# A two-layer recurrent and attention block: the first set-up reordered, k split by 128 channels in layer two, one relu moved

## The chip, the cores and the metric

One Trainium2 chip, one core. The metric is the device time of one execution in microseconds (us). TensorE (PE) multiplies, VectorE (DVE), ScalarE (ACT) and GpSimd (POOL) work on elements, SyncE (SP) issues most of the DMAs.

## The reference

Input x is 4 x 2048 rows of 256 channels. Two layers follow, each `x = x + s * silu(g)` with xn the layernorm of x.

Layer one, s: receptance, key and value are products of a mix of xn and the row before it with Wr, Wk, Wv; a recurrence runs over time for each channel:

```python
mo = jnp.maximum(m, kk + u)
e1 = jnp.exp(m - mo)
e2 = jnp.exp(kk + u - mo)
out = (e1 * num + e2 * vv) / (e1 * den + e2)
ms = jnp.maximum(m + w, kk)
e1s = jnp.exp(m + w - ms)
e2s = jnp.exp(kk - ms)
```

Then `sigmoid(receptance) * out` times Wo. Layer one, g: `relu(xn @ W1 + b1) @ W2 + b2` with 1024 hidden channels.

Layer two, s: latent attention with 16 heads of 16 channels and 8 rotary ones: c_q and c_kv are products of xn to 64 channels, q, k and v come from them, the scores are clipped and causal, and the result is multiplied by W_O. Layer two, g: `sigmoid(xr @ W_r) * (relu(xk @ W_k)^2 @ W_v)`, xr and xk being mixes of xn with its previous row.

## The kernel before

The 8192 rows are handled in 16 chunks of CH = 512 (4 to a batch row). The program has four stages, one after another: layer one with its set-up (0 to about 620 us), the projections of layer two with their set-up (to about 932), attention (to about 1940), and the output product. Each engine has its own instruction list, written out by hand, and waits on counting semaphores; the order in a list is the order of execution. Nearly all products are made of float16 halves: an operand is scaled and copied to a high half on ScalarE, and the rest, operand minus high half, is the low half, mostly on VectorE; a product is three matmuls (high x high, high x low, low x high).

Set-up of layer one. POOL computes the reciprocal deviation of each row (rstd_of). DVE squares and sums the three mixed weights (sum_squares), PE adds the sums over partitions with a product by ones (L804), ACT takes the root (L323), DVE makes the scales from it. Only then come, in ACT's list, normalise(0, 0) (four instructions, L382), xn_of(0, 0) (copies out of the transposed rows in ps_t: L346, and four of prev, L360), three weight_high (L333), two mixed_high (L375), and four squares with sums of the other weights (L455), whose sum over partitions (PE, L813) leads to a second root (L457) and second scales. DVE's list has xn_low_of(0, 0) (L522), mix(0) (four instructions, L511), weight_low 0 to 2 (L527), and two mixed_low (L517). PE's list: norm product L804, transposes(0) (L744), the receptance product behind w_low 3, norm product L813, key, value.

One chunk of layer one. ACT's chunk() takes the sigmoid of the receptance, then hidden(n, m), the relu of one of eight groups of 128 hidden channels (L399), with the three exponentials (L394; new, old, bonus) between them, and hidden_high (L404), the high halves. PE makes hidden product m into one of two halves of ps_a, so product m waits for relu m - 2. POOL makes the eight low halves (hidden_low, L278) and then the numerator's product with the sigmoid (L284). DVE runs keys() and states() with the scans over time (L544, L567 the denominator, L571 the numerator), takes rwkv (L696) and its low half (L699), which PE's output product (ps_out) waits for, and finishes the rows (L711, L713).

One chunk of layer two's projections. PE: latents, k of the relu branch (ps_b, behind xk_low), kr, qc, qr, transposes of the next chunk, receptance with k's up-projection in its middle (ps_c, `kc_mm`), values, and the squared-relu product (L1551), which waits for `kc_low` since it writes ps_c again. ACT: qc's high half (L1298), xn_of of the next chunk (L1236, prev copies L1250), with keys_high (L1302) in between. DVE: qr parts (L1442), layernorm statistics (L1338), k's low half (L1447), aggregate (L1345), xn's low half (L1350), mix (L1359), xk's low half (L1364), qr's low half (L1457), gate input (L1462). SP stores qc, kr, kc, qr, v and the gate in this order.

## Time and profile before

| | |
|---|---|
| Median of 3 runs | 2000.93 us (2000.35 to 2001.17) |
| Profiled execution | 2001.22 us, span 1999.5 us |
| PE busy in the span | 1893.0 us (95%) |
| DVE busy | 1765.7 us (88%) |
| ACT busy | 1710.3 us (86%) |
| POOL busy | 536.6 us (27%) |

The shares are means over stages with different limits, so they say little on a change in one stage. A row of a timeline gives the start in us from the span's start, how long it took, the engine, the line, the operation with its output and inputs, how many instructions are merged (xN), and in brackets how long the engine stood idle before it and who ended that.

### The profile page before, as it was taken

The page shows a single profiled execution, that of the slowest core. Times are in us where ns is not written, and L with a number is a line of the kernel's source. Part 1 is how long each engine was busy: PE and PEld are TensorE (multiplying, and loading weights), DVE is VectorE, ACT ScalarE, POOL GpSimd, SP SyncE. Part 2 cuts the span into 40 slices and gives each one's busy share as a digit, 9 for nine tenths or more (in the row PEclk, how much of TensorE's full clock was granted, in tenths as well). Part 3 has the DMA queues.
Part 4 walks back from the last instruction along what each step waited for, and adds up shares of the span by engine and source line. Part 5 has one row for each costly group of instructions (what it writes and reads, how often), then busy time and mean ns, then how long its engine had stood idle before and what let it go on. Part 6 is the DMA issues. An engine that isn't in the chain of part 4 may idle for free. (4 is left out here: it accounts for less than half of the span.)

```text
span 1999.5 us, 53552 instructions
## 1 busy us (share of the span) xinstructions
PE 1893.0 (95%) x22950; PEld 979.8 (49%) x22950; DVE 1765.7 (88%) x2361; ACT 1710.3 (86%) x2137; POOL 536.6 (27%) x426
## 2 busy tenths in 40 slices
PE   3899999999995999998999999999999999999988
PEld 1465665666653665664344433444344444344437
DVE  5999999999996888885898999989999899998976
ACT  6777877778775888886999999999999999999970
POOL 0564554646544676663000000000000000000003
PEclk9999999999997999998999999999999999999999
DMA  3001001010112465566222222222222222221329
GB/s 109 22 22 43 22 22 43 22 43 22 54 43 79 159 197 189 191 168 207 69 74 56 68 67 71 75 56 68 67 72 76 55 68 52 58 66 42 82 83 342
DMA packets 130221, 166.25 MB, mean 83 GB/s; under 512 B 13632, under 2 KB 101696, under 8 KB 129728
## 3 DMA queue, kind: packets, MB, share of 16 engines
q1 hardware_dynamic: 127952, 160.59, 27.3%
q8 instruction: 180, 2.95, 0.6%
q10 hardware_dynamic: 2032, 2.24, 0.3%
q14 instruction: 57, 0.47, 0.1%
HBM read 91.21 MB, written 71.57 MB: 81 GB/s over the span
## 5 line engine op out<-in xcount | busy, mean ns | idle before, releaser
L1771 ACT ACTIVATE c_probs<-c_ps_b 128x1536 f32<-128x1536 f32 x544 | 892.3, 1640 | 0.0
L1899 PE MATMUL c_ps_o<-c_probs,c_v 128*32 128x256 f32 (+3 forms) x6656 | 582.5, 453 | 3.7 <-DVE c_probs L1817 0.5
L1817 DVE TENSOR_SCALAR c_probs<-c_probs 128x2048 f32<-128x2048 f32 (+2 forms) x415 | 432.8, 1054 | 38.2 <-ACT c_probs L1771 36.2
L1879 PE MATMUL c_ps_b<-c_qk 24*128 24x256 f16 (+2 forms) x8064 | 459.8, 294 | 5.7 <-PEq L1099 5.7
L1879 PE MATMUL c_ps_a<-c_qk 24*128 24x256 f16 (+2 forms) x2688 | 449.9, 294 | 6.4 <-ACT c_probs L1770 4.9
L1770 ACT ACTIVATE c_probs<-c_ps_a 128x512 f32<-128x512 f32 x544 | 422.8, 777 | 2.5 <-PE c_ps_a L1879 2.5
L1879 PEld LDWEIGHTS c_ps_b<-c_qk 24*128 24x128 f16 x8064 | 222.7, 93 | 332.6 <-ACT c_probs L1771 243.9
L2052 POOL TENSOR_TENSOR d_prod<-d_prod,d_x 128x1024 f32<-128x1024 f32 x4 | 9.4, 2350 | 1025.5 <-DVE d_prod L2041 1025.5
L1899 PEld LDWEIGHTS c_ps_o<-c_probs,c_v 128*32 128x32 f32 x6656 | 161.7, 109 | 245.8 <-issue 146.6
L278 POOL TENSOR_TENSOR a_hidh<-a_hid,a_hidh 128x512 f16<-128x512 f32 x128 | 205.1, 1629 | 152.7 <-ACT a_hidh L404 152.7
L1879 PEld LDWEIGHTS c_ps_a<-c_qk 24*128 24x128 f16 x2688 | 199.4, 93 | 18.0 <-ACT c_probs L1770 15.3
L733 PE MATMUL a_ps<-a_xnh,a_w 128*128 128x512 f16 x768 | 175.6, 381 | 16.3 <-ACT a_hid L399 11.7
L1822 DVE TENSOR_SCALAR c_probs<-c_probs 128x1536 f32<-128x1536 f32 (+2 forms) x208 | 165.3, 801 | 28.5 <-ACT c_probs L1771 27.8
L733 PE MATMUL a_ps<-a_w,a_hidh 128*128 128x256 f16 x1536 | 171.3, 273 | 4.8 <-POOL a_hidh L278 4.8
L1826 DVE SCALAR_TENSOR_TENSOR c_probs<-c_probs,c_caps 128x512 f32<-128x512 f32 x256 | 169.5, 682 | 0.0
L733 PEld LDWEIGHTS a_ps<-a_w,a_hidh 128*128 128x128 f16 x1536 | 149.7, 98 | 27.4 <-POOL a_hidh L278 4.8
L733 PEld LDWEIGHTS a_ps<-a_xnh,a_w 128*128 128x128 f16 x768 | 71.8, 97 | 117.4 <-ACT a_hid L399 30.8
L399 ACT ACTIVATE a_hid<-a_ps,a_b 128x512 f32<-128x512 f32 x128 | 86.2, 688 | 18.9 <-PE a_ps L733 15.3
L733 PE MATMUL a_ps<-a_xnh,a_wr 128*128 128x512 f16 x384 | 87.5, 384 | 10.3 <-DVE a_wv L527 10.3
L1778 DVE STREAM_TRANSPOSE c_otok<-c_ps_o 128x512 f32<-128x512 f32 x64 | 45.9, 717 | 35.1 <-PE c_ps_o L1899 35.1
L404 ACT ACTIVATE a_hidh<-a_hid 128x512 f16<-128x512 f32 x128 | 75.2, 625 | 0.0
L375 ACT ACTIVATE a_xmixh<-a_xmix 128x1024 f16<-128x1024 f32 x32 | 33.8, 1057 | 40.6 <-DVE a_xmix L511 40.6
(278 smaller groups left out, 2795.9 us busy)
## 6 DMA issues: line engine op xcount, KB each, us to landing
v_d<-b_val SPq DMA_DIRECT2D x16, 1024.0 KB
c_v<-v_d SPq DMA_DIRECT2D x64, 256.0 KB
rows<-in_x SPq DMA_DIRECT2D x16, 512.0 KB, 4.8
x_d<-rows_out SPq DMA_DIRECT2D x16, 512.0 KB, 3.2
rows<-x_d SPq DMA_DIRECT2D x16, 512.0 KB, 5.1
qc_d<-b_qc SPq DMA_DIRECT2D x16, 512.0 KB
kc_d<-b_kc SPq DMA_DIRECT2D x16, 512.0 KB
gate_d<-rows_out SPq DMA_DIRECT2D x16, 512.0 KB, 3.3
```

The costliest lines, as they stand in the source:

```text
L278: nc.gpsimd.tensor_tensor(hid_half[:, 1, m], hid[:, m % RING], hid_half[:, 0, m], ALU.subtract).then_inc(hid_low, 1)
L399: nc.scalar.activation(hid[:, m % RING, :], ps_a[:, m % 2, :], ACT.Relu, bias=b_1[:, m:m + 1], scale=hid_scale).then_inc(hid_done, 1)
L404: nc.scalar.activation(hid_half[:, 0, m], hid[:, m % RING], ACT.Copy).then_inc(hid_high, 1)
L733: mm = nc.tensor.matmul(ps, l, r, start=(first and i == 0), stop=(last and i == len(steps) - 1))
L1770: nc.scalar.activation(probs[:, t % NPROB, PARTS[0]], ps_a[:], ACT.Exp, scale=unscale).then_inc(exp_a_done, 1)
L1771: nc.scalar.activation(probs[:, t % NPROB, PARTS[1]], ps_b[:, t % 2], ACT.Exp, scale=unscale).then_inc(exp_b_done, 1)
L1778: nc.vector.transpose(o_tok[:, e % 2].rearrange("p k r -> p (k r)"), ps_o[:]).then_inc(tok_done, 1)
L1817: nc.vector.tensor_scalar(tile, tile, P_MAX, P_MIN, ALU.min, ALU.max).then_inc(clip_done, 1)
L1822: nc.vector.tensor_scalar(tile[:, :, at:end], tile[:, :, at:end], P_MAX, P_MIN, ALU.min, ALU.max)
L1826: op = nc.vector.scalar_tensor_tensor(tile[:, :, at:at + P], tile[:, :, at:at + P], P_MIN, cap, ALU.max, ALU.min)
L1879: mm = nc.tensor.matmul(into, k[rows, hk, kt * P:(kt + 1) * P], tokens[rows, hq], start=(i == 0), stop=(i == len(TERMS) - 1), tile_positio ...
L1899: mm = nc.tensor.matmul(ps_o[j * VW:(j + 1) * VW, column:column + w], v[:, kt, j * VW:(j + 1) * VW], probs[:, step % NPROB, j, at:at + w], ...
```

## The change

Three places. In the set-up of layer one, ACT's root of the first norms comes after normalise(0, 0), PE's transposes(0) before the first norm product, DVE's weight_low(0) before mix(0), and PE's receptance waits for one low half of weights instead of three. In each chunk of layer one, relu 3 and one high half come ahead of the bonus exponential on ACT. In each chunk of layer two, the up-projection of k signals after each 128 channels, its high and low halves are taken per 128 channels, ACT's after one copy of prev instead of two, DVE's ahead of the next layernorm statistics; xn's low half moves ahead of the aggregation.

```diff
--- before.py
+++ after.py
@@ -319,9 +319,6 @@
                 act.dma_start(raw_1, a["W1"].rearrange("(k p) d -> p k d", p=P)).then_inc(ffn_loaded[0], 16)
                 act.dma_start(raw_2, a["W2"].rearrange("(m p) d -> p m d", p=P)).then_inc(ffn_loaded[1], 16)
 
-                act.wait_ge(sums_done, 1)
-                nc.scalar.activation(roots[:, 0:VAL], ps_a[:, 0, 0:VAL], ACT.Sqrt).then_inc(roots_done, 1)
-
                 def load(name, source):
 
                     register = act.alloc_register(name)
@@ -420,23 +417,27 @@
                     old_states(n, c)
                     if following:
                         xn_of(n + 1, c + 1)
-                    for m in range(3):
+                    for m in range(2):
                         hidden(n, m)
                         exponential(n, m)
+                    hidden(n, 2)
 
                     highs = 0
-                    for m in range(2, MT):
+                    for m in range(3, MT):
                         if first and m == MT // 2:
                             act.wait_ge(w_low, 5)
-                        if m > 2:
-                            hidden(n, m)
-                        if m in (2, 4, 5, 6):
+                        hidden(n, m)
+                        if m < MT - 1:
                             hidden_high(n, highs)
                             highs += 1
+                        if m == 3:
+                            exponential(n, 2)
                     for m in range(highs, MT):
                         hidden_high(n, m)
 
                 normalise(0, 0)
+                act.wait_ge(sums_done, 1)
+                nc.scalar.activation(roots[:, 0:VAL], ps_a[:, 0, 0:VAL], ACT.Sqrt).then_inc(roots_done, 1)
                 xn_of(0, 0)
                 act.wait_ge(scale_done, 1)
                 for i in range(3):
@@ -637,8 +638,9 @@
                 dve.wait_ge(bound_done, 2)
                 scales(slice(WR, W1), 2)
                 xn_low_of(0, 0)
+                weight_low(0)
                 mix(0)
-                for i in range(3):
+                for i in (1, 2):
                     weight_low(i)
                 mixed_low(0, 0)
                 mixed_low(0, 1)
@@ -798,16 +800,16 @@
                                           first=(m == 0 and j % 2 == 0), last=(m == MT - 1 and j % 2 == 1))
                     mm.then_inc(ffn_done, 1)
 
+                pe.wait_ge(small_loaded, 16 * 5)
+                transposes(0)
                 pe.wait_ge(consts_set, 5)
-
                 pe.wait_ge(squares_done, VAL)
                 nc.tensor.matmul(ps_a[:, 0, 0:VAL], ones[:], sums[:, 0:VAL], start=True, stop=True).then_inc(sums_done, 1)
-                pe.wait_ge(small_loaded, 16 * 5)
-                transposes(0)
 
                 pe.wait_ge(roots_done, 1)
+                pe.wait_ge(w_low, 1)
+                receptance(0, 0)
                 pe.wait_ge(w_low, 3)
-                receptance(0, 0)
                 pe.wait_ge(mix_done, len(MIXED) * KT)
                 pe.wait_ge(act_squared, COLUMNS - W1)
                 nc.tensor.matmul(ps_t[:, 0, 0:COLUMNS - W1], ones[:], sums[:, W1:], start=True, stop=True).then_inc(sums_done, 1)
@@ -1116,7 +1118,7 @@
                                  qc[:, s].rearrange("p h m t -> p (h m) t")).then_inc(stored[s], 16)
                     sp.wait_ge(kr_low, n + 1 + 1)
                     sp.dma_start(d["kr"][b, :, :, t].rearrange("h p t -> p h t"), kr[:, s]).then_inc(stored[s], 16)
-                    sp.wait_ge(kc_low, n + 1)
+                    sp.wait_ge(kc_low, KT * n + KT)
                     sp.dma_start(d["kc"][b, :, :, t].rearrange("h (m p) t -> p (h m) t", p=P),
                                  kc[:, s].rearrange("p h m t -> p (h m) t")).then_inc(stored[s], 16)
                     sp.wait_ge(qr_low, n + 1)
@@ -1249,8 +1251,8 @@
                         for k in range(KT):
                             nc.scalar.activation(prev[:, i, k, 1:CH + 1], ps_t[:, k, :], ACT.Copy,
                                                  scale=mix_prev[:, i, k:k + 1]).then_inc(prev_done, 1)
-                        if i and between:
-                            between()
+                            if i and k == 0 and between:
+                                between()
 
                 def xk_high_of(n, first=False):
                     act.wait_ge(mix_done, 2 * KT * n + KT)
@@ -1298,8 +1300,9 @@
                     nc.scalar.activation(qc[:, s, 0], ps_c[:], ACT.Copy, scale=q_factor).then_inc(qc_high, 1)
 
                     def keys_high():
-                        act.wait_ge(kc_mm, n + 1)
-                        nc.scalar.activation(kc[:, s, 0], ps_c[:], ACT.Copy, scale=k_factor).then_inc(kc_high, 1)
+                        for m in range(KT):
+                            act.wait_ge(kc_mm, KT * n + m + 1)
+                            nc.scalar.activation(kc[:, s, 0, m], ps_c[:, m], ACT.Copy, scale=k_factor).then_inc(kc_high, 1)
 
                     if left >= 1:
                         xn_of(n + 1, c + 1, keys_high)
@@ -1441,16 +1444,18 @@
                         dve.wait_ge(qr_mm, 2 * n + i + 1)
                         nc.vector.scalar_tensor_tensor(t_q[:], ps_a[:, i, :], factor[:, WQ:WQ + 1], table[:, t],
                                                        ALU.mult, ALU.mult).then_inc(qr_parts, 1)
+                    for m in range(KT):
+                        dve.wait_ge(kc_high, KT * n + m + 1)
+                        nc.vector.scalar_tensor_tensor(kc[:, s, 1, m], ps_c[:, m], factor[:, WUK:WUK + 1], kc[:, s, 0, m],
+                                                       ALU.mult, ALU.subtract).then_inc(kc_low, 1)
                     if left >= 2:
                         layernorm(n + 2, c + 2, b + (c + 2) // XS)
-                    dve.wait_ge(kc_high, n + 1)
-                    nc.vector.scalar_tensor_tensor(kc[:, s, 1], ps_c[:], factor[:, WUK:WUK + 1], kc[:, s, 0],
-                                                   ALU.mult, ALU.subtract).then_inc(kc_low, 1)
+                    if left >= 1:
+                        xn_low_of(n + 1)
                     if left >= 2:
                         dve.wait_ge(stats_done, TPC * (n + 2) + TPC)
                         aggregate(n + 2)
                     if left >= 1:
-                        xn_low_of(n + 1)
                         mix(n + 1, c + 1)
                         xk_low_of(n + 1)
                     dve.wait_ge(qr_high, n + 1)
@@ -1533,8 +1538,7 @@
                         if j == TPC // 2:
                             pe.wait_ge(qc_low, n + 1)
                             for m in range(KT):
-                                mm = products(ps_c[:, m, :], [(lambda h: w_uk[:, h, m * P:(m + 1) * P], lambda h: lat[:, 1])], both)
-                            mm.then_inc(kc_mm, 1)
+                                products(ps_c[:, m, :], [(lambda h: w_uk[:, h, m * P:(m + 1) * P], lambda h: lat[:, 1])], both).then_inc(kc_mm, 1)
                         mm = tokens(ps_r[:, j, :], xr_half, w_r, j)
                     mm.then_inc(r_mm, 1)
 
@@ -1543,7 +1547,7 @@
                         mm = products(ps_val[:, j, :], [(lambda h: lat[:, 1, j * P:(j + 1) * P], lambda h: w_uv[:, h])], ((0, 0), (0, 1)))
                     mm.then_inc(val_mm, 1)
 
-                    pe.wait_ge(kc_low, n + 1)
+                    pe.wait_ge(kc_low, KT * n + KT)
                     pe.wait_ge(act_done, n + 1)
                     pe.wait_ge(late_loaded, 48)
                     for j in range(TPC):
```

## Rows read from the trace of the kernel before

**Rows 1.** Busy us by engine (PE, PEld, DVE, ACT, POOL) in two stretches
```profile
80.00:120.00 40.00, 39.44 (x258) 24.79 (x256) 38.92 (x48) 32.37 (x47) 21.49 (x15) 1.00 0.09 27
720.00:760.00 40.00, 39.23 (x222) 24.07 (x222) 32.34 (x51) 32.82 (x47) 26.73 (x23) 1.00 0.56 186
```

**Rows 2.** Timeline of the set-up: start, us, engine, line, instructions, idle before
```profile
9.01 1.28 ACT L323 ACT_TABLE_LOAD   x1 [9.01 <-DMA rows_out<-in_WvT]
13.24 0.56 PE L804 MATMUL a_ps<-a_sums,a_ones 128*128 128x3 f32 x2 [13.24 <-DVE a_sums L596]
13.91 2.07 ACT L382 ACTIVATE a_xhat<-rows,a_shift,a_rstd 128x256 f32<-128x256 f32 x4
16.13 1.94 PE L744 MATMUL a_ps<-ident,a_xhat 128*128 128x128 f32 x8 [2.33 <-ACT a_xhat L382]
18.28 1.01 ACT L346 ACTIVATE a_xnh<-a_ps 128x1024 f16<-128x1024 f32 x1
23.01 2.72 DVE L511 SCALAR_TENSOR_TENSOR a_xmix<-a_ps,a_mix_now,a_prev 128x512 f32<-128x512 f32 x4
28.34 7.07 PE L733 MATMUL a_ps<-a_xnh,a_wr 128*128 128x512 f16 x24 [10.27 <-DVE a_wv L527]
31.83 0.18 ACT L455 ACTIVATION_READ_ACCUMULATOR a_hid<-a_rwkv 128x1 f32 x1
35.57 0.17 ACT L457 ACTIVATE a_roots<-a_ps 128x4 f32<-128x4 f32 x1 [3.56 <-PE a_ps L813]
```

**Rows 3.** Timeline, layer one: low half of rwkv, output product's first matmuls
```profile
80.50 1.22 DVE L699 TENSOR_TENSOR a_rwkvh<-a_rwkv,a_rwkvh 128x1024 f16<-128x1024 f32 x1
81.87 2.78 PE L733 MATMUL a_ps<-a_wo,a_rwkvh 128*128 128x256 f16 x24
115.95 1.22 DVE L699 TENSOR_TENSOR a_rwkvh<-a_rwkv,a_rwkvh 128x1024 f16<-128x1024 f32 x1
117.47 0.71 PE L733 MATMUL a_ps<-a_wo,a_rwkvh 128*128 128x256 f16 x5
578.72 1.23 DVE L699 TENSOR_TENSOR a_rwkvh<-a_rwkv,a_rwkvh 128x1024 f16<-128x1024 f32 x1
```

**Rows 4.** Timeline of one steady chunk of layer one
```profile
232.94 6.77 PE L733 MATMUL a_ps<-a_xnh,a_w 128*128 128x512 f16 x30
238.06 1.06 ACT L394 ACTIVATE a_eb<-a_eb 128x1024 f32<-128x1024 f32 x1
238.83 1.26 DVE L567 TENSOR_TENSOR_SCAN a_den<-a_eo,a_den,a_en 128x512 f32<-128x512 f32 x1
239.52 1.27 ACT L399 ACTIVATE a_hid<-a_ps,a_b 128x512 f32<-128x512 f32 x2
240.01 2.12 DVE L571 TENSOR_TENSOR_SCAN a_num<-a_eo,a_num,a_nv 128x512 f32<-128x512 f32 x1
240.27 4.08 PE L733 MATMUL a_ps<-a_xnh,a_w 128*128 128x512 f16 x18 [0.57 <-ACT a_hid L399]
241.39 1.69 POOL L278 TENSOR_TENSOR a_hidh<-a_hid,a_hidh 128x512 f16<-128x512 f32 x1 [0.34 <-ACT a_hidh L404]
```

**Rows 5.** Layer two: timeline of one chunk, then a line of the waits
```profile
743.28 1.27 ACT L1250 ACTIVATE b_prev<-b_ps,b_mix_prev 128x512 f32<-128x512 f32 x2
744.43 1.02 ACT L1302 ACTIVATE b_kc<-b_ps 128x1024 f16<-128x1024 f32 x1
745.49 1.28 DVE L1447 SCALAR_TENSOR_TENSOR b_kc<-b_ps,b_factor,b_kc 128x1024 f16<-128x1024 f32 x1
746.83 3.72 PE L1551 MATMUL b_ps<-b_wv,b_actk 128*128 128x256 f32 x16 [0.39 <-DVE b_kc L1447]
750.78 1.22 DVE L1364 TENSOR_TENSOR b_xkh<-b_xk,b_xkh 128x1024 f16<-128x1024 f32 x1
752.98 2.75 PE L1489 MATMUL b_ps<-b_xkh,b_wk 128*128 128x512 f16 x12
...
PE b_ps L1551 <- DVE b_kc L1447: 6.1, 16, 0.4
```

## The prediction

> **What bounds the kernel now.** I read the busy time by stretch first, then the set-up and one chunk of each layer in order of time. In the chunks of layer one TensorE is busy 39.44 of 40 us and VectorE 38.92; in those of layer two TensorE 39.23 of 40, with VectorE at 32.34 [rows 1]. Both loops stand on TensorE, with VectorE close behind in layer one only. The set-up is another regime: one chain that runs through ScalarE, VectorE and TensorE in turn [rows 2]. Attention and the output stage are not touched; I take their lengths as fixed and shift them. The sum is made against the profiled execution, 2001.22 us (span 1999.5); the median of the runs shown is 2000.93, so 0.3 us comes off at the end. A difference of 0.2% is 4 us, about what a measurement can tell from none.
>
> **Set-up of layer one.** Now: ScalarE's table is loaded at 9.01 + 1.28 = 10.29, but the four normalisations sit behind the square root that waits for the weight norms, and start at 13.91. The transposes run from 16.13 to 18.07, and the copy out of them starts at 18.28 [rows 2].
> Changed: the normalisations start at 10.3, 3.6 earlier. The transposes follow by the same 2.22 us, 12.5 to 14.5. The first norm product is now behind them: it starts near 14.35 instead of 13.24, and as ScalarE went on 0.67 after its start (13.91), it now has done the root by 15.0. The copies start at 15.2 instead of 18.28: 3.1 earlier. The later root costs nothing, since the scales it feeds are first used behind those copies, over 3 us later.
> Then the order on VectorE: the low half of the receptance weights (1.2 us, as the like instruction of 1.28 in [rows 5] with its 0.1 of overlap) moves ahead of the mix, so the mix, at 23.01, starts only 3.1 - 1.2 = 1.9 earlier. ScalarE's two copies of the mix and its squares follow it back to back, so the squares' end, 31.83 + 0.19, comes at 30.1. The receptance product (28.34, 7.07 us) needs only one weight now: it can start at 23.01 - 3.1 + 1.2 + 0.2 = 21.3 and ends at 28.4. Today the second norm product waits for that receptance (28.34 + 7.07 = 35.4, root at 35.57); afterwards it waits for the squares, so the root comes at 30.1 + 0.4 = 30.5. **Gain 5.0 us**, not the 7 that TensorE alone would show: what is late next are the squares. From the second root to the first chunk's sigmoid ScalarE has one unbroken queue, which shifts as a whole.
> Bounds: 4.7 if that tiny product takes the 0.67 of the first; 5.3 if I misplace one semaphore. An extra table load is possible, 1.28 us by the row. It would lie between 12.4 and 15.0, where ScalarE waits anyway: nothing; 1.3 if it came behind the wait.
> The Trainium skill (ScalarE: Activation LUTs, Table sets: the hidden batching unit) has the cheap functions in every set and the root in one of its own, which speaks for that extra load. Another section of the page (Step-by-step: what each stage is for) gives about 2.7 us for a load with its drain; by that the root would come 0.1 later, by the row's 1.28 not at all.
>
> **Relu 3 ahead of the bonus exponential.** In each steady chunk TensorE stands 0.57 us ahead of the sixth hidden product, for relu 3 [rows 4]. Five products take 6.77 us, 1.35 each, and end at 239.71; ScalarE starts relu 3 only at 239.52, behind the bonus exponential (238.06) and one high half, 1.46 us together. Moved ahead, relu 3 waits for its own product, the fourth, which ends at 238.36, and starts near 238.5; its reader can go 0.75 later (239.52 to 240.27 now), so that wait is gone. What is late next: relu 4, now behind high half and exponential. A relu costs 0.58 (two take 1.27): relu 4 starts at 238.5 + 0.58 + 1.46 = 240.54 and lets the seventh product go at 241.3, 0.2 to 0.3 after the sixth ends. TensorE gets 0.3 to 0.4 a chunk.
> It can't keep them. The output product waits for the low half of rwkv from VectorE. It started 1.37 us after that instruction's start where TensorE was early (80.50, 81.87), and 1.52 after it one chunk on (115.95, 117.47): only 0.15 of slack. And the one interval that begins with an early TensorE is 35.45 us (80.50 to 115.95); the 13 that follow, from 115.95 to 578.72, are 35.60 each [rows 3]. So VectorE's own loop is 35.45, and the gain is 0.15 x 13 = **1.9 us**. Bounds: 0, if the late relu 4 or a low half on GpSimd eats it; 5, if VectorE's loop got shorter too, for which no row speaks. In the first chunk and the last, VectorE and GpSimd bound these steps: nothing.
>
> **Layer two, k by halves.** TensorE stands 0.39 us a chunk ahead of the squared-relu product (L1551), for the low half of k; the waits come to 6.1 us in 16 [rows 5]. ScalarE takes k's high half at 744.43, after two copies of prev (1.15 for both), and VectorE the low half from 745.49 to 746.77. Changed: after one copy, at 743.86, the first 128 channels (I take 0.48 us to the next and 0.58 to its end, by half of the 1.02), done at 744.44. VectorE's halves start at 744.5 and 745.16, at 0.66 each, as the mix's instructions of that kind and size (2.72 for four, [rows 2]); they end at 745.9. The product can then start when TensorE is free, at 746.83 - 0.39 = 746.44: all 0.39 go, with 0.5 to spare.
> What is late next: VectorE. It filled the time up to 745.49 with the next rows' statistics; now it first waits for the half (0.36 more than it waits now), pays 0.12 for the second instruction, and the statistics follow. The low half of xn passes the aggregation and gains nothing, the mix gets nearly 0.5 later, and so does the low half of x_k: 750.78 + 0.46 + 1.22 = 752.46. Its reader, now at 752.98, moves to 752.59. It fits with 0.13, less some 0.06 for the semaphore. The 0.1 more on ScalarE lies in its waits. The store of k waits for both halves on SP's queue, behind kr's store, which GpSimd releases microseconds after them: nothing. All waits go: **6.1 us**. Bounds: 3, if each VectorE step comes 0.2 later than I place it; 6.5 at most.
>
> **The sum.** 5.0 + 1.9 + 6.1 = 13.0; 2001.2 - 13.0 - 0.3 = 1987.9, say 1988.0.
>
> **The rivals.**
> A: VectorE's delay in layer two takes the gain. If the low half of x_k comes 0.4 late, the new wait replaces the one removed and layer two gives 0 to 2: 1988.0 + 5 = 1993. For it: a margin of 0.07. Against: it needs an error of four times the steps I leave open.
> B, on the other side: the turns of GpSimd and VectorE flip in layer one. A scan alone takes 1.26; the first scan of the numerator takes 2.12 and the low half on GpSimd after it 1.69: they run one behind the other [rows 4]. Now low half 1 asks at 241.39 and starts in fact when the first scan is through, at 242.1 less 0.1. Its high half comes 0.45 later with the change, so it asks at 241.85. The point is 242.0: past it the second scan goes first, and GpSimd's whole chain ends one scan later, with the product for rwkv at its end, on which VectorE waits. 14 x 1.1 = 15.4 us come back: 1988.0 + 1.9 + 15.4 = 2005. Against: 0.15 us or more of margin in a loop that repeats itself to 0.02.
> The Trainium skill (SBUF — State Buffer, Terms) has these two engines share a port pair that is held for a whole instruction, the loser fully blocked. By that rule, the trace agrees (2.12 is the rest of a low half and then a scan). If they only shared bandwidth, no flip could happen and 2005 would fall away.
> C: TensorE's 0.3 to 0.4 a chunk in layer one are kept, as VectorE's loop shortens too: 13 x 0.2 more, 1985.
> D: the set-up gives less, since the normalisations still wait (a table load behind the root's wait, late statistics): the 5.0 fall to 1.2 to 3.7, and the time is 1990 to 1992.
>
> **The numbers.** Forecast 0.66 (its own range 1986.3 to 1990.3, by the bounds of its parts); A 0.12; B 0.07; C 0.06; D 0.05; something in attention's phase or at the joins of stages that I can't price 0.04. For eight in ten I reach to C and to A: 1985.5 to 1993. Faster by over 0.2% (under 1996.9): all but B and half of the last, less a little for A with D together, 0.88; within 0.2%: 0.04; slower: 0.08.
>
> **What would show it.** Set-up: normalisation at 10.3, receptance at 21.3, second root at 30.5. Layer one: no 0.57 wait before the sixth hidden product, one of 0.2 to 0.3 before the seventh, intervals of 35.45 throughout, and GpSimd's low half 1 still behind the first scan. Layer two: no wait at L1551, intervals of 17.4 instead of 17.8, and x_k's low half ending just ahead of its product. I am wrong if a wait for VectorE stands before the x_k product, if the intervals of layer one stay at 35.60 or exceed it, or if the second root comes after 31.

## The result and the profile after

The changed kernel takes 1986.1 us (median of 4 runs: 1984.7, 1984.8, 1987.5 and 1987.9) where the kernel before takes 2000.6: ratio 0.9929, 95% interval 0.9914 to 0.9944, so 14.5 us less. The forecast was 1988.0 with a range of 1985.5 to 1993. The profiled execution took 1984.83 us (span 1983.1), 16.4 less than the one profiled before.

**Set-up.** The timeline of the changed kernel, ScalarE's rows first, then TensorE's (columns as in [rows 2]):

```profile
9.10 1.28 ACT L379 ACT_TABLE_LOAD   x1 [9.10 <-issue]
10.40 2.08 ACT L379 ACTIVATE a_xhat<-rows,a_shift,a_rstd 128x256 f32<-128x256 f32 x4
12.49 1.28 ACT L440 ACT_TABLE_LOAD   x1
14.81 0.17 ACT L440 ACTIVATE a_roots<-a_ps 128x3 f32<-128x3 f32 x1 [1.04 <-PE a_ps L807]
14.99 1.01 ACT L343 ACTIVATE a_xnh<-a_ps 128x1024 f16<-128x1024 f32 x1
22.35 1.06 ACT L372 ACTIVATE a_xmixh<-a_xmix 128x1024 f16<-128x1024 f32 x1 [1.55 <-DVE a_xmix L512]
29.73 0.19 ACT L456 ACTIVATION_READ_ACCUMULATOR a_hid<-a_rwkv 128x1 f32 x1
30.46 0.17 ACT L458 ACTIVATE a_roots<-a_ps 128x4 f32<-128x4 f32 x1 [0.54 <-PE a_ps L815]
...
12.62 1.94 PE L746 MATMUL a_ps<-ident,a_xhat 128*128 128x128 f32 x8 [12.62 <-ACT a_xhat L379]
14.35 0.43 PE L807 MATMUL a_ps<-a_sums,a_ones 128*128 128x3 f32 x2
21.10 7.48 PE L735 MATMUL a_ps<-a_xnh,a_wr 128*128 128x512 f16 x24 [6.32 <-DVE a_wr L528]
30.07 0.36 PE L815 MATMUL a_ps<-a_sums,a_ones 128*128 128x4 f32 x2 [1.49 <-ACT a_hid L456]
```

Beside the rows of the kernel before [rows 2]: the normalisations start at 10.40 (13.91 before), the receptance at 21.10 (28.34), the second root at 30.46 (35.57). The last row names what is late next: TensorE has been through with the receptance for 1.49 us when the squares come. The extra table load (12.49) lies in ScalarE's wait.

**Layer one.** VectorE's product for the finished rows (the rows product), in the first chunk and in the last but one, of the kernel before and of the changed one. Then TensorE's weight loads in one chunk of the changed kernel, with what they waited for:

```profile
85.36 1.28 DVE L711 SCALAR_TENSOR_TENSOR rows_out<-a_ps,a_unscale,a_gate 128x1024 f32<-128x1024 f32 x1 [0.77 <-PE a_ps L733]
583.57 1.28 DVE L711 SCALAR_TENSOR_TENSOR rows_out<-a_ps,a_unscale,a_gate 128x1024 f32<-128x1024 f32 x1 [2.49 <-PE a_ps L733]
...
80.23 1.28 DVE L713 SCALAR_TENSOR_TENSOR rows_out<-a_ps,a_unscale,a_gate 128x1024 f32<-128x1024 f32 x1 [0.77 <-PE a_ps L735]
576.42 1.28 DVE L713 SCALAR_TENSOR_TENSOR rows_out<-a_ps,a_unscale,a_gate 128x1024 f32<-128x1024 f32 x1 [2.50 <-PE a_ps L735]
...
199.93 2.28 PEld L735 LDWEIGHTS a_ps<-a_xnh,a_w 128*128 128x128 f16 x12 [0.62 <-ACT a_hid L396]
209.31 3.83 PEld L735 LDWEIGHTS a_ps<-a_w,a_hidh 128*128 128x128 f16 x36 [0.33 <-POOL a_hidh L278]
218.49 2.53 PEld L735 LDWEIGHTS a_ps<-a_wo,a_rwkvh 128*128 128x128 f16 x24 [0.38 <-issue]
```

The first is 5.13 earlier and the second 7.15. So 5.13 us come from the set-up and 7.15 - 5.13 = 2.02 from the loop, whose interval went from 35.60 to 35.44 ([rows 3] for before). The matmuls' own wait of 0.57 ([rows 4]) is gone; what is late next is relu 4 (199.93), then GpSimd's low half 5 (209.31), then rwkv's low half (218.49, put down to "issue", 0.12 behind the end of that low half). From start to start of the hidden products, the sixth came 2.04 us after the fifth before, and 1.31 now, where 1.30 is the distance with no wait; the seventh now comes 1.59 after the sixth, so 0.29 late for relu 4.

**Layer two.** One chunk: two rows of TensorE in the kernel before, then ScalarE, VectorE and TensorE in the changed one.

```profile
745.41 1.04 PE L1489 MATMUL b_ps<-b_wuv,b_lat 128*128 128x256 f16 x8
750.39 2.75 PE L1489 MATMUL b_ps<-b_xnh,b_wc 128*128 128x512 f16 x12
...
732.44 1.08 ACT L1305 ACTIVATE b_kc<-b_ps 128x512 f16<-128x512 f32 x2
...
733.07 1.41 DVE L1449 SCALAR_TENSOR_TENSOR b_kc<-b_ps,b_factor,b_kc 128x512 f16<-128x512 f32 x2 [0.44 <-ACT b_kc L1305]
739.79 1.22 DVE L1367 TENSOR_TENSOR b_xkh<-b_xk,b_xkh 128x1024 f16<-128x1024 f32 x1
...
733.98 1.04 PE L1494 MATMUL b_ps<-b_wuv,b_lat 128*128 128x256 f16 x8
734.85 3.62 PE L1555 MATMUL b_ps<-b_wv,b_actk 128*128 128x256 f32 x16
738.31 2.75 PE L1494 MATMUL b_ps<-b_xnh,b_wc 128*128 128x512 f16 x12
741.11 2.75 PE L1494 MATMUL b_ps<-b_xkh,b_wk 128*128 128x512 f16 x12
```

Before, TensorE's steps started at 745.41 (values), 746.83 (squared relu, [rows 5]), 750.39 (latents) and 752.98 (k of the relu branch, [rows 5]). Taken from start to start of these steps: values 1.42, now 0.87; squared relu 3.56, now 3.46; latents 2.59, now **2.80**. That is 0.55 + 0.10 - 0.21 = 0.44 a chunk, the whole difference of the intervals (17.815, now 17.37), over 15 intervals 6.7 us. The wait of 0.39 was worth 0.65, and 0.21 came back as a new wait, for x_k's low half.

The pair of profiles shows 2.5 us more, at the joins of the stages. 1.53 of them lie in one place, the last output product of layer one: 4.33 us before, 2.79 after, at another clock of TensorE. Another 0.57 lie in the first two products of layer two, for the same reason (both below).

### The profile page after: what moved, and what is told of

It is laid out like the page before. It is cut to its first block and busy times, and to the rows that moved or that the text cites. A ratio compares the mean times of both kernels' runs of the same rounds, so it can differ in the third digit from the quotient of the medians.

```text
span 1983.1 us, 53585 instructions
## 1 busy us (share of the span) xinstructions
PE 1893.4 (95%) x22950; PEld 976.2 (49%) x22950; DVE 1766.1 (89%) x2377; ACT 1708.9 (86%) x2154; POOL 535.1 (27%) x426
```

## The experiments

Times are medians. The runs were made in three groups, each with the kernel before beside it: the three parts and experiment 2 (before: 2000.4); VectorE's old order, the late statistics, the early squares and the early table (2000.0); the whole low half, the one statistic, high half 0 and the joined kernel (2000.9). The interval is the distance of a loop's chunks in the trace. Every run is compared with the changed kernel's 35.44 in layer one and 17.367 in layer two, or with 35.60 and 17.815 of the kernel before.

**1. The parts alone.** Each of the three parts of the diff above, put into the kernel before by itself.

> The kernel before with the set-up part alone. My account of the result gives this part 5.1 us: the second root comes at 30.5 instead of 35.57, the first chunk's residual product at 80.3 instead of 85.4, and everything behind it is shifted by that: intervals of layer one stay at 35.60, those of layer two at 17.8, total 1995.5. Rival, that the parts only pay together (each frees what the next uses): the first product of the rows comes at 80.3 all the same but the layer's end moves by less than 4, total over 1996.5. Open besides: the full change gained 1.5 us in the last chunk of layer one, where the last output product took 2.79 us instead of 4.33 at another TensorE clock. If that is the place in time of the throttle, it can fall either way here, so the total may be 1994 to 1995.5.

Measured: 1994.8 (ratio 0.9973, 0.9963 to 0.9984). The first rows product is at 80.07, the intervals stay at 35.60 and 17.81. The last chunk's interval was 33.75, as in the changed kernel.

> The kernel before with relu 3 moved and nothing else. My theory: intervals between rows products of layer one go from 35.60 to 35.45 from the second on, 13 to 14 of them, 2.0 us, total 1998.6, and TensorE's wait ahead of the sixth hidden product (0.57) is gone while one of 0.3 for a low half of GpSimd's appears in the last stage of the chunk. Rival C: the gain per chunk is 0.3 to 0.4, 1996 or less. Rival: layer two or the set-up were needed for it, and the intervals stay at 35.60, 2000.6.

Measured: 1998.4 (0.9990, 0.9981 to 0.9999). Intervals 35.445, those of layer two 17.81; the last chunk's 35.42.

> The kernel before with k by halves in layer two and nothing else. My theory: the interval of layer two falls from 17.81 to 17.37, 15 x 0.44 = 6.6 us, total 1994.0; the wait ahead of the squared-relu product is gone and a gap of 0.5 appears ahead of the weights of the x_k product. Rival A: VectorE's later low half of x_k takes part of it back, interval 17.6, total 1997.5. Layer one keeps its 35.60.

Measured: 1994.2 (0.9966, 0.9954 to 0.9978). Interval 17.367, layer one as before, with 35.35 in its last chunk.

What follows: 5.65 + 2.05 + 6.24 = 13.9 of the 14.5. The parts add, and none needs another.

**2. Over the point of rival B.** In the changed kernel, high half 1 one relu later:

```diff
-                        if m < MT - 1:
+                        if m < MT - 1 and m != 4:
                             hidden_high(n, highs)
```

> The changed kernel with high half 1 one relu later, behind relu 5 instead of ahead of it, so that GpSimd's low half 1 asks after 200.9 in the chunk of 190 to 224 us where it asked at 200.39. This goes over the point that rival B of the prediction named (the end of the numerator's first scan, 200.87 there). Rival B's mechanism says: the second scan goes first, low half 1 starts at 202.0 instead of 200.9, GpSimd's chain and with it the product for rwkv come 1.1 later, intervals 36.5 instead of 35.45, 14 x 1.1 = 15 us, total 2001.5. My doubt: VectorE gets its second scan 1.0 earlier and GpSimd has waits in the chain that take part of it up, so the price may be 0.3 to 0.6 a chunk, 1990 to 1995. If the order of turns does not matter at all: 1986 to 1987.

Measured: 1990.7, against 1986.1 for the changed kernel; interval 35.81. The turns did flip. First VectorE and GpSimd of the changed kernel, then of this one, whose scans of the numerator begin 0.96 later:

```profile
198.82 4.15 DVE L572 TENSOR_TENSOR_SCAN a_num<-a_eo,a_num,a_nv 128x512 f32<-128x512 f32 x2
211.93 2.96 DVE L518 TENSOR_TENSOR a_xmixh<-a_xmix,a_xmixh 128x1024 f16<-128x1024 f32 x1
214.81 1.21 DVE L698 TENSOR_TENSOR a_rwkv<-a_on,a_od 128x1024 f32<-128x1024 f32 x1
...
200.47 11.01 POOL L278 TENSOR_TENSOR a_hidh<-a_hid,a_hidh 128x512 f16<-128x512 f32 x7 [0.61 <-ACT a_hidh L401]
211.45 2.35 POOL L284 TENSOR_TENSOR a_on<-a_on,a_sigr 128x1024 f32<-128x1024 f32 x1
```

```profile
199.78 3.29 DVE L572 TENSOR_TENSOR_SCAN a_num<-a_eo,a_num,a_nv 128x512 f32<-128x512 f32 x2
212.01 1.77 DVE L518 TENSOR_TENSOR a_xmixh<-a_xmix,a_xmixh 128x1024 f16<-128x1024 f32 x1
216.04 1.22 DVE L698 TENSOR_TENSOR a_rwkv<-a_on,a_od 128x1024 f32<-128x1024 f32 x1 [2.25 <-POOL a_on L284]
...
202.10 10.60 POOL L278 TENSOR_TENSOR a_hidh<-a_hid,a_hidh 128x512 f16<-128x512 f32 x7 [1.29 <-ACT a_hidh L401]
212.66 3.35 POOL L284 TENSOR_TENSOR a_on<-a_on,a_sigr 128x1024 f32<-128x1024 f32 x1
```

Low half 1 starts only at 202.10, when the second scan has begun (201.82), and no longer holds it up: the two scans take 3.29 instead of 4.15. In the changed kernel it started at 200.47, 0.40 ahead of the second scan. GpSimd's chain ends at 216.01 instead of 213.80 + 0.96 = 214.76, 1.25 later. But rwkv starts at 216.04 instead of 215.77, only 0.27 later: VectorE's low half of the mix (L518) was held up behind the numerator's product (2.96 for a step of 1.77 here and 1.2 alone), and now goes ahead of it. So rival B's mechanism is real, and its point lies where it was put, between these two requests. Its price is 0.37 a chunk, not 1.1 (0.27 here, 0.10 ahead of the scans): what takes up the rest is a second change of turns further down.
The Trainium skill (SBUF — State Buffer, Terms) calls the two engines' shared port pair an exclusive lock for the whole instruction. These rows agree: a step lasts either its own time or about that plus the rest of the other engine's step. GpSimd's product takes 2.35 alone and 3.35 here, where L518 has 1.12 left as it starts.

**3. Order or split in layer two.** The kernel before, with k's halves and ScalarE's early turn, but VectorE's old order.

```diff
                     if left >= 2:
                         layernorm(n + 2, c + 2, b + (c + 2) // XS)
-                    dve.wait_ge(kc_high, n + 1)
-                    nc.vector.scalar_tensor_tensor(kc[:, s, 1], ...
+                    for m in range(KT):
+                        dve.wait_ge(kc_high, KT * n + m + 1)
+                        nc.vector.scalar_tensor_tensor(kc[:, s, 1, m], ...
```

> The kernel before with k's high and low halves per 128 channels and ScalarE's early turn for them, but VectorE in its old order (statistics, low halves of k, aggregation, low half of xn). VectorE's statistics ended near 745.1 and it then waited for the high half until 745.49; now the half is there, so its low halves run from about 745.1 to 746.5 instead of 745.49 to 746.77. By my theory that is the split and ScalarE's order alone: the wait of 0.39 ahead of the squared-relu product shrinks to 0.05 to 0.15, and the low half of x_k comes earlier than before, so this variant gets 0.25 to 0.35 a chunk, interval 17.5, total 1995.5 to 1996.5, where the whole part gave 17.367 and 1994.2. If instead VectorE's new order is what carries the part, the interval stays near 17.8 and the total near 2000.

Measured: 1997.7, interval 17.71.

```profile
741.93 1.40 DVE L1339 BATCH_NORM_STATS2 b_stats<-rows 128x6 f32<-128x256 f32 x4
743.25 1.39 DVE L1449 SCALAR_TENSOR_TENSOR b_kc<-b_ps,b_factor,b_kc 128x512 f16<-128x512 f32 x2
...
744.69 3.72 PE L1552 MATMUL b_ps<-b_wv,b_actk 128*128 128x256 f32 x16 [0.29 <-DVE b_kc L1449]
```

I had expected 17.5. The low halves start when the statistics end, and end at 744.64; TensorE still waits 0.29. The early half on ScalarE is worth 0.10 a chunk as long as VectorE does its statistics first.

The other way round, the changed kernel with VectorE's new order but one low half for all channels, behind both high halves:

```diff
-                    for m in range(KT):
-                        dve.wait_ge(kc_high, KT * n + m + 1)
-                        nc.vector.scalar_tensor_tensor(kc[:, s, 1, m], ...
+                    dve.wait_ge(kc_high, KT * n + KT)
+                    nc.vector.scalar_tensor_tensor(kc[:, s, 1], ...
```

> The changed kernel with k's low half as one instruction behind both high halves, everything else as changed (ScalarE's early turn, VectorE's order). It asks what the halves are worth beside the order. The low half then starts at 733.57 instead of 733.07 and ends 0.35 later, at the time when TensorE wants it (734.85), and everything behind it on VectorE comes 0.37 later, the low half of x_k too, which TensorE already waits for. My theory, that VectorE's chain is the bound of the changed layer two: 0.37 a chunk, interval 17.7 to 17.8, total 1992. Rival, that only the order matters: interval 17.37 to 17.45, total 1987 or less.

Measured: 1989.6, interval 17.725. As my theory had it: VectorE waits 0.93 instead of 0.44 for ScalarE, and TensorE's latents last 3.02 from start to start (741.82 to 744.84) instead of 2.80; the squared-relu product starts 0.05 late and lasts 0.10 more. Of the 0.445 a chunk, the halves with VectorE's old order give 0.10, and VectorE's new order with one whole low half (ScalarE keeps its halves and its early turn) gives 0.09: the order and VectorE's halves are each worth some 0.35 only where the other is there.

**4. Is VectorE the bound of the changed layer two?** The changed kernel with all statistics and the aggregation behind x_k's low half.

```diff
-                    if left >= 2:
-                        layernorm(n + 2, c + 2, b + (c + 2) // XS)
                     if left >= 1:
                         xn_low_of(n + 1)
...
                         mix(n + 1, c + 1)
                         xk_low_of(n + 1)
+                    if left >= 2:
+                        layernorm(n + 2, c + 2, b + (c + 2) // XS)
+                        dve.wait_ge(stats_done, TPC * (n + 2) + TPC)
+                        aggregate(n + 2)
```

> The changed kernel with VectorE's statistics and aggregation of the next rows behind the low half of x_k in layer two. My reading of the changed kernel: its x_k product stands 0.21 us (741.11 where the latents' last matmul lets it start at 740.90) for x_k's low half, so VectorE is the new bound there. Then this takes 0.2 a chunk off: interval 17.37 to 17.15, 15 x 0.2 = 3.0, total 1983. Rival: TensorE's own work is 17.37 and the 0.21 is its sequencer: interval and time stay (1986). Other rival: the later aggregation delays GpSimd's root and ScalarE's normalisation by 1 us, and the transposes or the squared relu behind them: interval over 17.4, total over 1986.5.

Measured: 2004.1, interval 18.68, 1.3 a chunk slower. My theory missed the total by 21 us, and the second rival held, of which I had thought little.

```profile
732.63 2.08 ACT L1232 ACTIVATE b_xhat<-rows,b_shift,b_rstd 128x256 f32<-128x256 f32 x4 [2.22 <-POOL b_shift L1169]
736.46 1.01 ACT L1300 ACTIVATE b_qc<-b_ps 128x1024 f16<-128x1024 f32 x1
...
737.50 1.28 DVE L1441 SCALAR_TENSOR_TENSOR b_qc<-b_ps,b_factor,b_qc 128x1024 f16<-128x1024 f32 x1 [2.12 <-ACT b_qc L1300]
...
738.84 1.04 PE L1493 MATMUL b_ps<-b_lat,b_wuk 128*128 128x512 f16 x4 [1.00 <-DVE b_qc L1441]
745.69 2.75 PE L1493 MATMUL b_ps<-b_xnh,b_wc 128*128 128x512 f16 x12
748.28 1.89 PE L1493 MATMUL b_ps<-b_xkh,b_wk 128*128 128x512 f16 x8
```

The late statistics make ScalarE wait 2.22 for GpSimd's root ahead of the normalisation; qc's high half is queued behind it, VectorE waits 2.12 for that, and TensorE 1.00 for qc's low half. But its last two rows answer the question: with x_k's low half done at 747.39, 0.89 ahead of its reader, the latents last 748.28 - 745.69 = 2.59. The 0.21 of the changed kernel is VectorE's.

So the remedy is smaller: only the first of the four statistics goes ahead, into VectorE's own wait of 0.44 (layernorm is given the range of statistics to take).

```diff
+                    if left >= 2:
+                        layernorm(n + 2, c + 2, b + (c + 2) // XS, range(1))
                     for m in range(KT):
                         dve.wait_ge(kc_high, KT * n + m + 1)
...
                     if left >= 2:
-                        layernorm(n + 2, c + 2, b + (c + 2) // XS)
+                        layernorm(n + 2, c + 2, b + (c + 2) // XS, range(1, TPC))
```

> The changed kernel with the first of the four statistics of the next rows ahead of k's low halves in layer two, where VectorE waits 0.44 us for ScalarE's first high half. The earlier variant with all statistics late showed the x_k product start 2.59 behind the latents (748.28 - 745.69) where the changed kernel needs 2.80 (741.11 - 738.31), so the gap of 0.21 is VectorE's. Here 0.33 of its work moves into its own wait, so x_k's low half ends 0.33 earlier and the 0.21 go: interval 17.37 to 17.16, 14 to 15 x 0.21 = 3.0, total 1983. Rival: the statistic takes longer than the wait and the low halves of k come later, so that the squared-relu product waits again: interval 17.37 to 17.5.

Measured: 1983.0 (0.9912, 0.9897 to 0.9927), interval 17.162:

```profile
731.66 0.41 DVE L1341 BATCH_NORM_STATS2 b_stats<-rows 128x6 f32<-128x256 f32 x1
732.19 1.41 DVE L1451 SCALAR_TENSOR_TENSOR b_kc<-b_ps,b_factor,b_kc 128x512 f16<-128x512 f32 x2
...
737.43 2.75 PE L1496 MATMUL b_ps<-b_xnh,b_wc 128*128 128x512 f16 x12
740.02 2.32 PE L1496 MATMUL b_ps<-b_xkh,b_wk 128*128 128x512 f16 x10
```

Latents 2.59, the 0.21 are gone, and the low halves of k are not late.

**5. Are the squares late next in the set-up?** The changed kernel with ScalarE's squares of b1 and Wo ahead of the mix's high halves (mixed_high), W1's and W2's behind. square() is the body of the old loop.

```diff
+                square(b_1[:], HID, small_loaded)
+                square(raw_o, WO, raw_o_loaded)
                 mixed_high(0)
+                square(raw_1, W1, ffn_loaded[0])
+                square(raw_2, W2, ffn_loaded[1])
```

> The changed kernel with ScalarE's squares of b1 and Wo ahead of the mix's two high halves (ScalarE waits there for 1.55 us ahead of 22.35). By the prediction what is late next in the set-up are the squares: their end comes 1.2 earlier (30.07 to 28.9), behind the receptance product's end at 28.6, the second root comes at 29.2 to 29.3 instead of 30.46, and the total falls by 1.2: 1985. If the first chunk were set by something else (the weights' halves, the receptance), the root comes earlier and the first rows product at 80.23 stays. The last chunk of layer one may again take 1.5 us more or less with TensorE's clock.

Measured: the second root at 29.11 and the first rows product at 79.19, 1.35 and 1.04 earlier. The median, 1985.9, doesn't separate it from the changed kernel's 1986.1: a gain of 1 us is below what these runs tell, and the traces alone show it. In the eight profiles with the new set-up and the old order of squares the first rows product lies at 79.95 to 80.41, in the two with the early squares at 79.19 and 79.03 (experiment 7).

**6. What does layer one's 35.44 stand on?** The changed kernel with the sigmoid's table loaded behind the reciprocal (L408), where ScalarE waits 2.40 us.

```diff
                     nc.scalar.activation(out_den[:], out_den[:], ACT.Exp, scale=-1.0).then_inc(rden_done, 1)
+                    act.preload_act_table_set("sigmoid_and_others")
```

> The changed kernel with ScalarE's table for the sigmoid loaded right behind the reciprocal's exponential, where ScalarE waits 2.4 us, instead of between the high half of rwkv and the gate's sigmoid. This asks what layer one's loop of 35.44 stands on, now that relu 3 is out of the way. The trace names TensorE's output product for VectorE's wait of 0.77 ahead of L713, but GpSimd's gate product ends at 221.91, 0.1 ahead of L713 at 222.01, and TensorE's output product at 221.3. If the gate is what VectorE waits for: its sigmoid starts at 217.3 instead of 218.43, the gate is ready by 221.0, L713 starts with the output product at 221.4, and the interval falls by 0.3 to 0.6: 35.0, total 1980. If the output product is what it waits for, the interval stays at 35.44 and the total at 1986.

Measured: 1984.9, interval 35.43: no gain in the loop, where I had expected 0.3 to 0.6 a chunk if the gate was what VectorE waits for.

```profile
196.40 2.46 DVE L569 TENSOR_TENSOR_SCAN a_den<-a_eo,a_den,a_en 128x512 f32<-128x512 f32 x2
221.76 1.28 DVE L714 SCALAR_TENSOR_TENSOR rows_out<-a_ps,a_unscale,a_gate 128x1024 f32<-128x1024 f32 x1 [0.58 <-PE a_ps L736]
...
218.33 3.34 POOL L290 TENSOR_TENSOR a_gate<-a_gp 128x1024 f32<-128x1024 f32 x1 [4.58 <-ACT a_gp L413]
```

The gate's sigmoid did come 1.2 earlier, but GpSimd's product then takes 3.34 instead of 2.35, since it asks while VectorE is in a two-input instruction of its own (L519, 218.24 to 219.46); it ends at 221.67, and the rows product starts 0.1 behind it as before (222.01 behind 221.91). The output product had ended at 221.30 there, 0.7 ahead. So the gate, not the output product that the row names, is what VectorE waits for. The 0.2 that are left of the gain are lost at the denominator's scan: it starts at 196.40, as exp_old ends at 196.36, 1.37 behind the instruction ahead of it (195.03), which it follows by 1.20 in the changed kernel. In the changed kernel the exponential ended at 196.40; 0.04 behind it, as here, is 196.44, and the scan started at 196.46, so there the two were ready within 0.02 of each other. VectorE's loop ties with a second one, through TensorE's transposes and ScalarE's exponentials. No run shortens this second one, so what the loop would gain by that is not shown.

High half 0 ahead of relu 3, in the changed kernel:

```diff
                     hidden(n, 2)
+                    hidden_high(n, 0)
 
-                    highs = 0
+                    highs = 1
...
-                        if m < MT - 1:
+                        if 3 < m < MT - 1:
```

> The changed kernel with high half 0 ahead of relu 3 in layer one, so that ScalarE's wait of 0.17 ahead of relu 3 (197.15) is used and GpSimd's first low half can ask near 197.4 instead of 198.4. My present reading of layer one's loop of 35.44: it runs through ScalarE's second exponential, the scans and the run of low halves behind them, so that an earlier relu 4 alone gives nothing: 35.3 to 35.5, total 1984 to 1987. Rival, TensorE is the bound (it waits 0.6 for relu 4's weights): interval 35.27, total 1983.7. Other rival, GpSimd's low half 0 now falls between the denominator's scans and delays the whole run of turns: over 35.6, total over 1989.

Measured: 1985.6, interval 35.486. TensorE's eight hidden products went from 10.80 to 10.53 us from first start to the next stage, and the stage behind them from 10.70 to 11.02: TensorE's part of the gain is given back in full, for GpSimd's low halves. TensorE's own work isn't the bound of the changed loop.

**7. What pays, together:** the squares, the one statistic and the table.

> The changed kernel with the squares of b1 and Wo early, one statistic ahead of k's low halves, and the sigmoid's table behind the reciprocal. If the parts add: 1.1 + 3.0 + 0.2 = 4.3 us, total 1981.8, ratio to the kernel before 0.9909. Less, over 1983, if the statistic doesn't give its 3.0.

Measured: 1981.3 (ratio to the kernel before 0.9903, 0.9888 to 0.9918), the fastest of all; rows product at 79.03, intervals 35.425 and 17.162.

## Why the prediction was right, step by step

**Set-up, 5.0:** 5.13 in the pair of profiles, 5.65 by the medians of the part alone. Every step came within 0.2: normalisation 10.3 said and 10.40 found, copies 15.2 and 14.99, receptance 21.3 and 21.10, root 30.5 and 30.46. The squares were late next, as experiment 5 shows by moving them. The table load lay in the wait and cost nothing, and rival D's wait of the normalisations did not come. The difference of 5.13 and 5.65 is for the most part TensorE's clock, a term that the prediction didn't have. In the old set-up the second root waits for the receptance product, and from that product's start to the root four profiles show 7.23, 7.19, 7.94 and 7.94 us: its granted clock rises from 1.2 to 2.4 GHz 3.52, 3.45, 4.98 and 4.96 us after that start, behind an idle time of TensorE of some 10 us. The new root waits for the squares instead and no longer depends on it. The first rows product lies at 85.36 to 86.14 in the four old profiles and at 79.95 to 80.41 in the eight new ones, on average 5.65 earlier; the pair of the forecast had one of the quicker old ones.

**Relu 3, 1.9:** 2.02. The one interval of the kernel before that began with an early TensorE (35.45) gave the number. The reason I put behind it, "VectorE's own loop is 35.45", is only half of it: VectorE has 0.77 of idle time in each such interval, and shortening that gives nothing (experiment 6), since the scans then wait for a chain through TensorE and ScalarE that is as long to within 0.02. Rival C, TensorE's time kept, was wrong: the interval is 35.44, and in experiment 6 (high half 0) a further 0.27 of TensorE's time is given back whole. The forecast of 0.3 to 0.4 for TensorE was right in its parts: 0.29 late at the seventh product (0.2 to 0.3 said), 0.45 gained in the hidden products. Of that 0.22 went ahead of low half 5, which I had not named, and 0.07 ahead of the output product.

**Layer two, 6.1:** 6.7, out of two terms of the wrong size that cancel in part, so the closeness of the sum is some luck. The wait was priced at its idle time, 0.39. It cost 0.65: the idle time is counted from the modelled end of the last matmul, which lies 0.17 behind the moment at which the next one starts when nothing waits (1.04 for the eight matmuls, 0.87 to the next start), and the product behind a wait took 3.72 instead of 3.62. Against it, "it fits with 0.13" failed by 0.3: x_k's low half began at 739.79, and TensorE, now earlier by 0.65 and not by 0.39, waited 0.21 for it. With 0.65 in place of 0.39, the margin of 0.07 turns to -0.19: the sum of the prediction, made with the right price, gives the wait that was found. So rival A was there: it took back 0.21 of the 0.65.

**Rival B:** the request of low half 1 comes at 200.39, 0.48 ahead of the second scan's start (200.87) and not 0.15 as I had it (relu 4 came 0.15 earlier than said, the high half behind it 0.27). The point held; the price was three times too high (experiment 2).

**The rest of 14.5.** The three parts explain 13.9. The profiled pair shows 16.4, but 1.5 of it is TensorE's clock in one product, which the change has no part in: the last output product of layer one takes 2.79 us in ten of the 14 profiles and 4.33 to 4.46 in four. The kernel before and the kernel with VectorE's old order (experiment 3) have the same layer one and fell on either side, with 4.33 and 2.79. So did the kernel with the whole low half (experiment 3) and the changed kernel, whose layer one is the same too. The rows are the product in the kernel before, in the kernel with the whole low half with a window of time within it, and in the changed kernel with the same window (columns of a window: its start and end, its length, busy us of PE, PEld, DVE, ACT and POOL, granted clock, DMA's busy share and GB/s):

```profile
614.49 4.33 PE L733 MATMUL a_ps<-a_wo,a_rwkvh 128*128 128x256 f16 x24 [2.51 <-DVE a_rwkvh L699]
...
607.00 4.46 PE L735 MATMUL a_ps<-a_wo,a_rwkvh 128*128 128x256 f16 x24 [2.51 <-DVE a_rwkvh L701]
```

```profile
607.80:611.00 3.20, 3.20 (x17) 2.28 (x15) 0.00 (x0) 0.00 (x0) 1.52 (x1) 0.50 0.00 0
```

```profile
607.35 2.79 PE L735 MATMUL a_ps<-a_wo,a_rwkvh 128*128 128x256 f16 x24 [2.51 <-DVE a_rwkvh L701]
```

```profile
607.80:611.00 3.20, 2.35 (x22) 1.85 (x19) 0.82 (x1) 0.00 (x0) 1.87 (x1) 1.00 0.00 0
```

In the window the granted clock is 0.50, that is 1.2 GHz, in the one and 1.00, 2.4 GHz, in the other. In both TensorE had waited 0.31, twice 0.61 and then 2.51 us in the stretch ahead.

Of the remaining 1 us, 0.57 is the clock again. The first two products of layer two, behind an idle time of 10.17 us, take 7.94 us from start to start before (640.83 to 648.77) and 7.37 after (632.15 to 639.52): the granted clock rises from 1.2 to 2.4 GHz 5.4 us into them in the one and 4.3 in the other. Without these two places the profiled pair shows 14.3.

## What to carry to other kernels

Price a wait of TensorE from start to start of its groups, against a chunk in which nothing waits, not by its idle time; here that was 0.65 for an idle time of 0.39 (and in layer one 0.74 for 0.57), and it decides whether what comes later on the other engines is still in time. Where one engine waits in its own list, the cheapest remedy is a piece of its own later work that just fills the wait (one statistic of four, 3 us), while moving all of it delayed a chain through three other engines (18 us). In a loop where two engines take turns on a shared resource, the shift of one request is neither free nor additive: follow the turns to the step that all wait for before a price is put on a flip.

## What the runs showed of the hardware that I had not expected

The product behind a wait is longer itself, by 0.10 us (3.72 instead of 3.62), in the kernel before and in both of experiment 3, in the second of which it started only 0.05 late (0.92 behind the values' start instead of 0.87).
The Trainium skill (TensorE: Matmul & The Clock Gate, Step-by-step: what each phase is for) has consecutive matmuls hide the fill and drain of the array, which speaks for such a price; it names none for a group, and no run here separates the cause.

TensorE's granted clock fell to 1.2 GHz either within the last output product of layer one or only behind it, with the same code and the same waits ahead. That is 1.6 us by chance, as far as these runs show. Its rise in the old set-up and at the start of layer two moved too, for up to 0.8 and 0.6 us. So a gain of 1 us, as in experiment 5, is read from one stage of the trace and not from the total.

From the start of a table load to the start of the activation behind it 1.30 us passed (9.10 to 10.40). Within the loop of the changed kernel the load started 0.01 behind the end of the activation ahead of it (217.12 and 217.13), and the next activation 0.02 behind the load's end (218.43). Of the 2.7 us of the Trainium skill (ScalarE: Activation LUTs, Step-by-step: what each stage is for), which the prediction had weighed, no part beyond the 1.28 shows here.
